# Two attention and mixture layers on one core: operand parts moved inside SBUF, and more products on TensorE at the start

## The reference

```
xn = layernorm(x)
x  = x + attention0(xn) + gated_ffn0(xn)     # 16 heads of 8 numbers, softmax over 512 keys, int weights / 127
xn = layernorm(x)
x  = x + attention1(xn) + moe1(xn)           # the same heads with a block mask; 8 experts, the best 2, with a capacity
```

## Time and profile before

| | us |
|---|---|
| median of 3 runs | 523.88 (523.43 to 524.0) |
| the profiled execution | 523.32 |
| its span, first to last instruction | 521.1 |
| TensorE, VectorE, ScalarE, GpSimd busy | 454.9, 396.2, 331.9, 266.5 |

### The profile page before, as it was taken

One profiled execution on the slowest core, in us unless ns is written; L12 is line 12 of the kernel. 1 busy time (PEld: TensorE's weight loads), 2 busy tenths in 40 slices (PEclk: granted clock), 3 DMA queues, 4 the chain that ended last, 5 costly groups with the idle time before them and its releaser, 6 DMA issues.

```text
span 521.1 us, 9480 instructions
## 1 busy us (share of the span) xinstructions
PE 454.9 (87%) x3442; PEld 177.3 (34%) x3442; DVE 396.2 (76%) x554; ACT 331.9 (64%) x439; POOL 266.5 (51%) x503
## 2 busy tenths in 40 slices
PE   3555989999999999999999988987999999999962
PEld 1201223324432443243424222221245453555512
DVE  3499889996999699969996988888886777723304
ACT  2301677776677677757776777767766657577570
POOL 6782085724535473787388758874202233163434
PEclk9855899999999999999999999999999999999995
DMA  3797439534820361636162636355721111010025
GB/s 86 223 237 109 75 115 269 152 147 150 175 87 20 124 62 20 64 124 87 20 67 81 119 40 64 120 92 70 97 55 36 42 54 50 2 48 20 31 82 189
DMA packets 140734, 48.27 MB, mean 93 GB/s; under 512 B 109954, under 2 KB 135058, under 8 KB 139858
## 3 DMA queue, kind: packets, MB, share of 16 engines
q1 hardware_dynamic: 138386, 42.93, 39.3%
q0 software_dynamic: 2304, 4.76, 2.7%
HBM read 22.81 MB, written 23.14 MB: 88 GB/s over the span
## 4 chain that ended last, share of the span: by engine, by line
PE 59%; DVE 17%; ACT 9%; issue 8%; DMA 3%; POOL 2%; SPq 1%; ACTq 0%; DVEq 0%; POOLq 0%
PE ps L808 16%; DVE mx L1194 11%; PE ps L792 10%; PE ps L777 8%; ACT PT L1034 6%; PE ps L849 3%; PE ps L735 3%; PE ps L857 3%; PE ps L832 3%; PE ps L850 2%; PE ps L872 2%; PE ps L833 2%; PE ps L869 2%; PE ps L816 1%; POOL y_tokens L550 1%
## 5 line engine op out<-in xcount | busy, mean ns | idle before, releaser
L1194 DVE TENSOR_REDUCE mx<-ps 128x2 f32<-128x1024 f32 x256 | 307.6, 1220 | 57.6 <-PE ps L777 54.2
L1034 ACT ACTIVATE PT<-ps 128x1024 f32<-128x1024 f32 x256 | 258.6, 1025 | 107.6 <-PE ps L792 101.7
L808 PE MATMUL ps<-PT,Vp 128*32 128x512 f32 x1024 | 137.9, 608 | 4.5 <-ACT PT L1034 4.4
L777 PE MATMUL ps<-KO,QO 48*128 48x512 bf16 (+1 forms) x512 | 103.9, 403 | 32.1 <-ACT PT L1034 15.9
L792 PE MATMUL ps<-QO,KO 59*128 59x512 bf16 x512 | 99.9, 388 | 1.3 <-DVE mx L1194 1.1
L550 POOL DMA_INDIRECT y_tokens<-expert_io,meta x40 | 38.4, 961 | 67.5 <-ACT expert_io L1069 50.2
L792 PEld LDWEIGHTS ps<-QO,KO 59*128 59x128 bf16 x512 | 24.5, 93 | 137.2 <-issue 74.9
L1216 DVE SCALAR_TENSOR_TENSOR th<-th,ps 128x320 f32<-128x320 f32 (+1 forms) x56 | 25.5, 455 | 31.9 <-ACT th L1054 31.6
L777 PEld LDWEIGHTS ps<-KO,QO 48*128 48x128 bf16 (+1 forms) x512 | 25.6, 96 | 61.7 <-ACT PT L1034 28.8
L538 POOL DMA_INDIRECT x_places<-xe,place_i x32 | 31.8, 993 | 20.0 <-ACT PT L1034 14.4
L587 POOL CAST mp<-mx 128x32 bf16<-128x32 f32 x16 | 3.4, 211 | 71.9 <-DVE mx L1194 67.9
(11 more groups left out here) (168 smaller groups left out, 491.3 us busy)
## 6 DMA issues: line engine op xcount, KB each, us to landing
z<-part SPq DMA_DIRECT2D x16, 384.0 KB, 2.6
z<-part SPq DMA_DIRECT2D x16, 256.0 KB, 3.0
QO<-z SPq DMA_DIRECT2D x64, 48.0 KB, 2.7
KO<-z SPq DMA_DIRECT2D x64, 48.0 KB, 2.6
x_places<-expert_io SPq DMA_DIRECT2D x2, 1300.0 KB, 7.2
expert_io<-x_places SPq DMA_DIRECT2D x8, 320.0 KB, 3.7
QO<-z SPq DMA_DIRECT2D x6, 384.0 KB
KO<-z SPq DMA_DIRECT2D x6, 384.0 KB
```

The source lines that it names most:

```text
L777: mm = pe.matmul(ps[:, 2 * pair + half, :], rows_of(QO[u % 3], half, 2 * s + jj, rows, (qt, qt + 1)), rows_of(KO[u % 3], half, 2 * s + jj, ...
L808: last = pe.matmul(ps[32 * g:32 * g + 32, PV_BANK, :], Vp[u % 2][:, k, head(s, g), :], PT[:, (2 * t + g % 2) % 4, g // 2, :], start=(s % 2 ...
L1034: act.activation(PT[:, e % 4], ps[:, 2 * pair:2 * pair + 2, :], ACT.Exp).then_inc(exp_done, 1)
L1194: dve.tensor_reduce(mx[:, a, qt, col:col + 5:4], ps[:, 2 * pair:2 * pair + 2, :], AX_X, ALU.max, negate=True).then_inc(max_read, 1)
```

## The change

It has two halves. In layer 0 the parts go from `part` straight to `QO` and `KO`: one transfer for a slot and a half of the heads, from 64 partitions to 8, with 8 heads side by side, 64 KB. That is 12 a side and 24 a unit. For unit 0, SP issues those of parts 0 and 2, ScalarE those of part 1; for the other units SP issues all. To make a head's rows lie as the transfer wants them, the columns of the weights and biases for Q and K are sorted in another way by the host (`halves_first`). `max_mms` waits for all 24 at once, and GpSimd's `parts` for units 1 to 4 waits until all 24 of the unit before have landed, both sides. Layer 1 keeps the way through DRAM.

In the other half TensorE gets products whose results nobody reads: 18 transposes of the identity ahead of the first transposes, 2 behind them, and one product of 512 columns (`clock_mm`) beside each of the 24 pairs for the first maxima. The product for the value bias is moved ahead of the transposes of sequence 1, and the wait for its addition from behind the maxima to before the first `clock_mm`.

```diff
-            return 16 * sum(4 if layer(v) == 0 else 16 for v in range(u % 3, u + 1, 3))
+            return 16 * sum(24 if layer(v) == 0 else 16 for v in range(u % 3, u + 1, 3))
...
+        def operand_moves(eng, p, side, i):
+            if p >= 3:
+                eng.wait_ge(exp_done, 32 * (p - 2))
+            eng.wait_ge(part_ready[side], 3 * p + i + 1)
+            for slot in range(*SLOTS[i][side]):
+                for half in range(2):
+                    lo = 64 * half + 8 * slot
+                    eng.dma_start((QO, KO)[side][p % 3][lo:lo + 8], part[i][64 * half:64 * half + 64, side, :]).then_inc(
+                        qk_rows[p % 3], 16)
...
-            if p >= 1:
-                eng.wait_ge(z_written[side], 16 * Z_WRITES * p)
+            if 1 <= p <= B:
+                eng.wait_ge(qk_rows[(p - 1) % 3], reads_of(p - 1))
+            elif p > B:
+                eng.wait_ge(z_written[side], 16 * Z_WRITES * (p - B))
...
+        def clock_mms(pe, n):
+            for _ in range(n):
+                pe.transpose(ps[:, 0, 0:P], ident[:], ident[:])
...
-                if u == 0:
-                    pe.wait_ge(first_rows[0], 16 * 4)
-                else:
-                    pe.wait_ge(qk_rows[u % 3], reads_of(u))
+                pe.wait_ge(qk_rows[u % 3], reads_of(u))
...
+        def clock_mm(pe, q):
+            if q == 0:
+                pe.wait_ge(v_bias_added, 1)
+            s, qt, jj = q // 8, q % 8 // 2, q % 2
+            pe.matmul(ps[:, PV_BANK, :], rows_of(QO[0], 0, 2 * s + jj, PROD_ROWS, (qt, qt + 1)),
+                      rows_of(KO[0], 0, 2 * s + jj, PROD_ROWS, (0, NT)), start=True, stop=True)
...
@@ sync
-            operand_writes(sp, 0, 0)
-            operand_writes(sp, 0, 1)
-            first_reads(sp)
+            for i in (0, 2):
+                for side in range(2):
+                    operand_moves(sp, 0, side, i)
...
-            operand_writes(sp, 1, 0)
-            operand_writes(sp, 1, 1)
-            operand_reads_0(sp, 1)
+            for side in range(2):
+                for i in range(3):
+                    operand_moves(sp, 1, side, i)
@@ scalar
             xnT_copy(act, 1, SIDE)
+            for side in range(2):
+                operand_moves(act, 0, side, 1)
@@ tensor
+            clock_mms(pe, 18)
             xnT_mms(pe, 0, SIDE)
+            clock_mms(pe, 2)
...
             v_mms(pe, 0, 5)
+            value_bias(pe)
             xnT_mms(pe, 1, SIDE)
...
             for q in range(20):
                 max_mms(pe, q)
+                clock_mm(pe, q)
```

More of the change, by code:

```diff
@@ L198, in build @@
         z_written = [sem(f"z_written{side}") for side in range(2)]
-        first_rows = [sem(f"first_rows{i}") for i in range(2)]
         qk_rows = [sem(f"qk_rows{i}") for i in range(3)]
@@ L407, in store @@
             sp.dma_start(out[b].rearrange("(t p) d -> p t d", p=P), out_tile(B + b)[:]).then_inc(stored, 16)
+        def operand_moves(eng, p, side, i):
[7 more added lines that the diff above has]
+                        qk_rows[p % 3], 16)
         def operand_writes(sp, p, side):
-            if p >= 2 and side == 0:
+            if p >= B + 2 and side == 0:
                 sp.wait_ge(qk_rows[(p - 2) % 3], reads_of(p - 2))
[L412 to L416, removed]
+                sp.wait_ge(late_rows[(p - 2) % 3], late_reads_of(p - 2))
             for i in range(3):
@@ L423, in operand_writes @@
                     z_written[side], 16)
[L425 to L444, removed]
         def operand_reads_1(sp, p, a):
@@ L482, in sync_unit @@
             if p < U:
-                operand_writes(sp, p, 0)
-                operand_writes(sp, p, 1)
+                for side in range(2):
+                    if layer(p) == 1:
+                        operand_writes(sp, p, side)
+                    else:
+                        for i in range(3):
+                            operand_moves(sp, p, side, i)
                 if u < 2:
@@ L487, in sync_unit @@
                         sp.dma_start(dst, src).then_inc(experts_loaded, 16)
-                if layer(p) == 0:
-                    operand_reads_0(sp, p)
-                else:
+                if layer(p) == 1:
                     operand_reads_1(sp, p, 0)
@@ L1537, in _ @@
             qk_mm(pe, 1, 1, SIDE)
-            value_bias(pe)
             pe.wait_ge(v_read, 1)
@@ L1546, in _ @@
                 max_mms(pe, q)
-            pe.wait_ge(v_bias_added, 1)
+                clock_mm(pe, q)
             pe.wait_ge(mT_ready, 1)
@@ L1568, in dims_first, with halves_first @@
         return np.ascontiguousarray(np.swapaxes(a.reshape(16, 8, -1), 0, 1).reshape(a.shape))
+    def halves_first(a):
+        a = np.asarray(a)
+        return np.ascontiguousarray(np.swapaxes(a.reshape(2, 8, 8, -1), 1, 2).reshape(a.shape))
     def heads_grouped(a):
@@ L1581 @@
         "x": np.asarray(L0_attn_x),
-        "wq": np.stack([T(dims_first(qkv_w[0:128])), T(dims_first(L1_attn_Wq))]),
-        "wk": np.stack([T(dims_first(qkv_w[128:256])), T(dims_first(L1_attn_Wk))]),
+        "wq": np.stack([T(halves_first(qkv_w[0:128])), T(dims_first(L1_attn_Wq))]),
+        "wk": np.stack([T(halves_first(qkv_w[128:256])), T(dims_first(L1_attn_Wk))]),
         "wv": np.stack([T(qkv_w[256:384]), T(blocks_last(L1_attn_Wv))]),
-        "bq": np.stack([dims_first(qkv_b[0:128]), dims_first(L1_attn_bq)]),
-        "bk": np.stack([dims_first(qkv_b[128:256]), dims_first(L1_attn_bk)]),
+        "bq": np.stack([halves_first(qkv_b[0:128]), dims_first(L1_attn_bq)]),
+        "bk": np.stack([halves_first(qkv_b[128:256]), dims_first(L1_attn_bk)]),
         "bv": np.stack([heads_grouped(np.tile(qkv_b[None, 256:384], (128, 1)))[:, 0], blocks_last(L1_attn_bv)]),
```

7 lines of the change are left out of this document (1 added, 6 removed).

## The result

| | before | changed |
|---|---|---|
| median | 523.61 us (523.4 to 524.0, 5 runs) | 542.99 us (542.64 to 544.76, 5 runs) |
| profiled execution, its span | 523.32, 521.1 | 543.91, 541.4 |

The changed kernel is slower, by the ratio 1.0376 with its interval [1.0362, 1.0389]: 19.4 us. The forecast was 525.8 with a range to 532.5, so the sign was right and the time lies far outside. The parts of the prediction that named the place (the beginning) were right; the size of one term was not, and one loss was named by none.

The account below looks back on a forecast made before the run. Bound: two transfers and VectorE's row maxima in the beginning, TensorE in each unit's body. Terms -1.2 + 4.0 + 0.4 - 1.3 = +1.9 us, so 525.8 us; own range 524.3 to 527.5, unconditional 519.4 to 532.5.

Parts of the forecast that it names:

- What bounds the kernel: Beginning: two transfers, then VectorE's 25 row maxima (28.38 us), then TensorE; only a shifted beginning or a later hole moves the end.
- The moves, +4.0: Unit 0's start: issues at 0.78 us, landing 2.45 + 0.35, together 14.5 against 11.45 us, plus 0.9 for crowding.
- The rival of narrow destinations: Moves into few partitions queue up, from about 1 us each; chances 0.10 near 532 us and 0.06 near 568.
- SP is held back: Expected sign of slow narrow moves: SP issues of 1.2 us and more, with mT's rows waiting behind them.
- its two cases, 532 and 568: Slow narrow moves: at 0.95 us each +8 us, 532 (chance 0.10); at 1.33 us each +44, 568 (chance 0.06).
- Before the layer norm, -1.2: Start of unit 0: added transposes warm TensorE's clock, Q product from 2.05 to 1.13 us; -1.2, bounds 0 and -1.8.
- the rival by which transposes don't warm the clock: Start of unit 0: the -1.2 us goes and the rest stays, +3.1, 527.0 us; chance 0.18.
- GpSimd and mT's rows, +0.4: Unit 1's parts wait for the first maximum, mT's rows go out later behind SP's moves; +0.4 us, bounds 0 and +2.5.
- Products beside the maxima, -1.3: Added 512-column products fit, delay nothing and lift the clock before the first value products; -1.3 us, bounds 0 and -1.6.
- Nothing in later units: Units 2 and 3 of layer 0: moves cost nothing at 0.78 us each; no gain named past the first unit.

## Why the prediction was wrong, point by point

*What bounds the kernel.* Right: 14.2 of 19.4 us lie ahead of VectorE's first maximum, and VectorE's 28.4 us and the units behind it pass them on unchanged.

*The moves, +4.0.* This step failed: the time of a move behind its issue. "2.45 us; 64 KB instead of 12 add an estimated 0.35" and 0.9 for crowding: from the last issue to the landing it was 15.03 us. From the first move's issue to the first product it was 25.8 us, where the sum had 14.5 and 0.9, so the term is +14.4 and not +4.0. The issues were as the sum had them, a little quicker (0.71 for 0.78). The 2.45 came from mT's rows, of 12 KB, one pair at a time. The evidence for the rest was in the same text: zero and key rows at 59 GB/s with the DMA engines half busy. The sum set it aside with "Here source partitions are spread and neighbours go to other partitions", and the runs show that a source spread over 64 partitions doesn't help as long as the eight of the destination are neighbours. (A narrow source with a spread destination wasn't tried.) A small slip beside it changes nothing: from 72.26 to 74.75 it is 2.49, not 2.45. Where it is spread too, the step holds almost to the digit: 2.70 us from the last issue to the landing, where it had 2.80, and the first product at 25.46.

*The rival of narrow destinations.* Its mechanism was right and so was its price: 1.07 us a move measured (12.87 to 38.52 for 24), between its 0.95 and 1.33. What it took for its sign was wrong, "SP is held back". The queues took 16 and then 24 moves, none of them issued in more than 0.84 us by SP (the issue behind the sixteenth, of constants, took 1.30). For that reason the losses it put on units 1 to 3 didn't come (mT's rows of unit 0 went out 22.23 us after the first maximum's product, 21.80 before), and the measured time lay between its two cases, 532 and 568.

*Before the layer norm, -1.2.* Half right. The K product of unit 0 took 1.02 us in the changed kernel, and 1.91 or 1.92 in the five profiles without the transposes (with them it was 1.02 to 1.17 in eight, 1.62 to 1.91 in three). The granted clock reads 1.00 there in both kernels, so that this rests on the durations alone. But the Q product ahead of it was often still slow, 1.97 in the changed kernel, 2.05, 1.42 and 1.10 in others with the same start, so that part 0 came 0.2 to 1.8 us earlier. That speaks against the rival by which transposes don't warm the clock, without showing when they do. The Trainium skill, page TensorE: Matmul & The Clock Gate, section Part 4: PE-mode transpose, has it that they don't count as TensorE being busy in the same way; the durations speak against it, 1.02 against 1.92 in most profiles (the 44 one-column products at the start left it at 1.92).

*GpSimd and mT's rows, +0.4.* GpSimd began unit 1's parts at 38.64, right at the first maximum, as said, and mT's rows were 0.43 us later against it, as said. It cost nothing: from VectorE's first maximum to the first value products it was 29.64 us, 29.63 before.

*Products beside the maxima, -1.3.* Wrong: they fit and delayed no maximum, but left the clock at 0.50.

*Nothing in later units.* Wrong by 3.7 us in unit 4, and by a cause that no row of before could price: the number of instructions on TensorE, and with it the place of a transfer of its list. Another 1.0 us in unit 1 stays open.

Two steps by two edits lead from 542.99 to 525.38: 4.9 for the count and then 12.7 for neighbouring partitions, or in the other order 14.9 and then 2.7. The two are not independent, as the pause costs 2.2 us less with the rows apart. The 525.38 that is left is 1.8 us above before, and that the sum had 1.9 is luck: nothing was gained beside the maxima, where it had 1.3, and in the profile the maxima began 2.1 us late (27.27 for 25.15) by way of ScalarE's issues and the 84 products behind them, where it took ScalarE's issues as hidden.

## What to carry to other kernels

When many transfers write a few neighbouring partitions, spread these, where the order of the rows is free: it costs one slice with a step (528.08 for 542.99 here). A queue hides its length from the engine that fills it, so take the price of a transfer from GB/s over a stretch at a known DMA share, not from its issue or from the landing of a single small one. And where an edit adds or removes instructions on a busy engine, measure it beside a version with the same number of idle ones, and look where the transfers on the instruction queue fall, or a pause far off is booked as the edit's effect.

## What was not expected of the hardware

- Eight neighbouring partitions took 75 GB/s at a DMA share of 0.49, eight partitions six apart 128 GB/s at 0.44, in the same number of pieces: 132 and 46 ns for a piece of 1 KB. Sixteen neighbouring ones had pieces of 125 ns, but about twice as many at once.
- 88 more TensorE instructions without work cost 2.4 us (1.0053), and with 256 more there was no such loss: the pause opens behind 128 products of 32 columns when a transfer of instructions begins among them, and TensorE goes on 1.31 to 1.47 us after its end. Pauses of 1.46, 1.94 and 2.02 us were followed by some 3 us at 1.2 GHz, those of 0.99, 1.30 and 1.42 were not.
- TensorE fully busy for 5 us with products of 128 columns on 128 rows under the maxima kept the granted clock at 0.50; with transposes of the identity before the first real work the K product took 1.02 to 1.17 us in eight of eleven profiles, without them 1.91 or 1.92 in all five.
- The same transposes gave a Q product of 1.10, 1.42 or 2.05 us in different executions.
